# Three conditioned transformer blocks on one core: scores of two heads as row tiles, keys moved by POOL's queue, softmax sums spread inside SBUF

## The chip, the cores and the metric

The kernel runs on one core of a Trainium2 chip. A core has TensorE (PE: matmuls, with a separate load of the stationary operand), VectorE (DVE), ScalarE (ACT), GpSimd (POOL) and SyncE (SP, used here only to start transfers); each follows its own instruction stream, and they meet at semaphores. SBUF holds the working data in 128 partitions, PSUM the matmul results in banks of 2 KB per partition. The metric is the device time of one execution in microseconds.

## The reference

A batch of 16 sequences of 256 tokens with 288 channels, and a condition vector for each. First a rotation of the tokens in a 64-dimensional subspace (the exponential of a skew matrix made from the condition). Then three blocks of one form, with their own weights, all in float32:

```python
ada = silu(c) @ W_ada + b_ada
shift_a, scale_a, gate_a, shift_f, scale_f, gate_f = split(ada, 6)
h = layernorm(x) * (1 + scale_a) + shift_a
q, k, v = split_heads(h @ W_qkv + b_qkv)            # 16 heads of 18 channels
p = softmax(q @ k.T * 18 ** -0.5)                   # 256 x 256 for each head
x = x + gate_a * (merge(p @ v) @ W_proj + b_proj)
h = layernorm(x) * (1 + scale_f) + shift_f
x = x + gate_f * (gelu(h @ W_fc1 + b_fc1) @ W_fc2 + b_fc2)   # hidden width 1152
```

## The kernel before, in words

`prepare` (lines 56 to 1007) computes rotations and modulations, until about 168 us. `layers` then runs 48 half-steps, one for each batch element `b` and layer `l`, with `it = 16 l + b`. Each engine has its own `half_step`, a fixed order written out by hand, and the same four kinds of work lie side by side in it: softmax and weighted values of `it`, QKV and scores of `it + 1`, the norm of `it + 2`, and projection and MLP of `it - 1`.

Products that need float32 accuracy are made of three float32r products of high and low parts (`split`, `channel_steps`): ScalarE or VectorE writes the rounded high part, POOL or VectorE the low part (`low`, L1411). So `qk[0]` and `qk[1]` hold queries and keys of all heads as high and low parts, five tiles of 7 x 18 rows.

Scores need both parts in one contraction. Transfers therefore copy pieces into stacks: `q_stack` holds for a pair of heads (a unit, eight of them) three 36-row pieces (high, low, high), 108 rows; `k_stack` holds the pieces high, high, low for each of the two heads with zeros where the other head's rows are, so it is twice as wide. SP issues all 24 transfers of a half-step (`stacks`): three for queries and six for keys of units 0 to 4 (semaphore `s_stack_a`, after shifted unit 4 of the half-step has been computed), nine and six for units 5 to 7 (`s_stack_b`, after shifted unit 7).

- `score_unit` (L1819): for 128 queries at a time one matmul over 108 rows and 512 columns, both heads at once. VectorE reduces each unit to row maxima (`unit_max`, L2070), which TensorE transposes (L1829); ScalarE negates them, and SP and ScalarE copy them into rows 108 and 109 of `q_stack`, where ones in `k_stack` meet them.
- `shifted_unit` (L1842): keys by queries, four matmuls over 110 rows and 256 columns, the maxima already subtracted. ScalarE takes the exponential of the whole unit (L1604). Two units are in flight, in the two PSUM tiles `scores`.
- `weighted_values` (L1856): four heads as column tiles of 32, with a column of ones that gives the softmax sums in rows 18, 50, 82, 114. ScalarE copies the result to `o_full` (L1611).
- The sums: ScalarE issues a store to DRAM (`gather_sums`, L1618) before GELU 0 and a load into `sums`, 128 partitions of 32 (`load_sums`, L1623), behind it. VectorE takes the reciprocal, ScalarE stores it and issues four broadcasts into `inv_sum`. VectorE writes `o_full * inv_sum` rounded to `o_att[0]` (L2082), POOL computes the same product in full (L1481) and subtracts (L1411) for `o_att[1]`. The projection of the next half-step waits for that.
- The MLP: up-projections 0 to 4 (L1881) alternate between two PSUM banks; GELU `n` makes `g_full` (L1646) and `hidden[0]` (L1647), and up `n + 2` waits for it. `down` (L1736) follows in six parts, with score units between them.

TensorE's order in a half-step: projection of `it - 1` with the maxima's transposes, QK tiles 0 to 2 with shifted units 0 to 2 between, shifted 3, MLP transposes, shifted 4, weighted values 0 and 1, shifted 5 and 6, values 0, shifted 7, up 0, weighted values 2 and 3, up 1, values 1, up 2 and 3, score unit 0, up 4, score unit 1, transposes of `it + 2`, then down parts with score units 2 to 7 between.

Of the kernel before, what the change touches and what calls it, by code (L numbers as in the profile page):

```python
# [12 lines left out]
P = 128  # L13
# [25 lines left out]
PAIR_ROWS, SHIFTED_ROWS = 6 * HD, 6 * HD + 2  # L39
# [20 lines left out]
def prepare(nc, dram, keep, early):  # L60
# [10 lines left out]
    with ExitStack() as ctx:  # L71
# [264 lines left out]
        def _(act):  # L336
# [26 lines left out]
            def constant_stacks():  # L363
# [5 lines left out]
                for u in (0, 4):  # L369
                    A(k_stack[:, u:u + 4, :, :].rearrange("p u n t -> p (u n t)"),  # L370
                      one[:, 0:1].to_broadcast([P, 8 * T]), ACT.Copy, scale=0.0).then_inc(early["s_kinit"], 1)

            def constant_rows():
                act.wait_ge(early["s_kinit"], 2)
                act.wait_ge(s_ident, 16)
                k_stack, rows = early["k_stack"], slice(P - 32, P)
                for par in range(2):
                    for u in (0, 4):
                        A(k_stack[rows, u:u + 4, par, :], one[rows, 0:1].unsqueeze(2).to_broadcast([32, 4, T]), ACT.Copy,
                          scale=ident[rows, PAIR_ROWS + par:PAIR_ROWS + par + 1]).then_inc(early["s_kinit"], 1)  # L380
# [72 lines left out]
            for k in range(PHASES):  # L453
# [3 lines left out]
                if k == 1:  # L457
                    constant_rows()
# [551 lines left out]
def layers(nc, dram, keep):  # L1010
    dram["sum_scratch"] = nc.dram_tensor("sum_scratch", (4, 2 * 512), F32, kind="Internal").ap()

    ident, mods = keep["ident"], keep["mods"]
    with ExitStack() as ctx:  # L1014
# [20 lines left out]
        k_stack = sb("k_stack", [P, H // 2, 2, T], F32R)  # L1035
# [34 lines left out]
        s_stack_b = sem("s_stack_b")  # L1070
        s_v_ps = sem("s_v_ps")
# [10 lines left out]
        s_sum_st = sem("s_sum_st")  # L1082
# [5 lines left out]
        s_o_norm = sem("s_o_norm")  # L1088
# [42 lines left out]
        def qkv_order(tile, rows_as_given):  # L1131
# [3 lines left out]
            if rows_as_given:  # L1135
                pairs = qk_part.rearrange("p (b c) -> p b c", c=PAIR)
                return [pairs[:, 0:5, :], pairs[:, 8:13, :], pairs[:, 5:7, :], pairs[:, 13:16, :],
                        pairs[:, 7, :].rearrange("p (a c) -> p a c", c=HD), tile[:, 2 * C:3 * C]]
            tiles = qk_part.rearrange("p (m c) -> p m c", c=QK_ROWS)
            return [tiles[:, 0:5, 0:PAIR], tiles[:, 0:5, PAIR:2 * PAIR], tiles[:, 0:2, 2 * PAIR:3 * PAIR],  # L1140
                    tiles[:, 2:5, 2 * PAIR:3 * PAIR], tiles[:, 0:2, 3 * PAIR:QK_ROWS], tile[:, V_START:IN_COLS]]

        def conversion(n, rows, part=None):
# [4 lines left out]
            blocks = slice(0, 6) if part is None else slice(0, 5) if part == "qk" else slice(5, 6)  # L1148
# [76 lines left out]
        def qk_rows_of(m):  # L1225
            return QK_ROWS if m < 2 else 3 * PAIR
# [1084 lines left out]
```

## Time and profile before

| | |
|---|---|
| median of 3 runs | 2104.65 us (2098.85 to 2105.66) |
| the profiled execution | 2105.64 us, span 2103.9 us |
| mean granted clock of TensorE | 0.969 |
| busy: PE, PE loads | 1967.8 us (94%), 1754.2 us (83%) |
| busy: DVE, ACT, POOL | 1210.3, 1120.0, 1003.5 us |
| `unit_max` L2070 | 384 of 1222 ns |
| exponentials L1604 | 384 of 1027 ns |
| score matmuls L1819, shifted L1842 | 768 and 1536 |
| POOL's full product L1481 | 96 of 1479 ns |
| transfer packets on POOL's queue | 2256, 7.17 MB |

Busy times are the union of an engine's instructions; issues of transfers are not counted in them. Matmuls are pipelined, so a matmul's duration (0.28 us for one of 256 columns) is longer than the distance between two of them, and the distance between starts, or between ends, is what one costs. "Idle before" says how long an engine stood still and what released it. A granted clock of 1.00 is 2.4 GHz, 0.5 is 1.2 GHz.

### The profile page before, as it was taken

What the parts mean: (1) busy time and instruction counts of PE and PEld (TensorE: products, weight loads), DVE (VectorE), ACT (ScalarE), POOL (GpSimd) and SP (SyncE); (2) the same over time, 40 slices, a digit from 0 to 9 for tenths busy, and PEclk for the clock granted to TensorE, in tenths of its full rate; (3) what the DMA queues carried; (4) which work ended last, traced back from release to release, by engine and by line L of the source; (5) the groups of instructions that cost most, each with busy time, mean ns of one, the idle gap of its engine ahead of it and who ended that gap; (6) DMA issues with size and microseconds to landing.
All of it is one profiled execution on the core that took longest, in us unless ns stands there. A gap on an engine that the chain in (4) does not pass through costs nothing. (4 is left out here: it accounts for less than half of the span.)

```text
span 2103.9 us, 49860 instructions
## 1 busy us (share of the span) xinstructions
PE 1967.8 (94%) x16599; PEld 1754.2 (83%) x16599; DVE 1210.3 (58%) x2720; ACT 1120.0 (53%) x1932; POOL 1003.5 (48%) x1031
## 2 busy tenths in 40 slices
PE   4785799999999999899999999999999999999997
PEld 2553589999899988789899899998789998998986
DVE  6874466546556475556556465575565565564641
ACT  4232455564655645554655656645555656656552
POOL 1002345545455554645455454554655554554534
PEclk9797899999999999999999999999999999999998
DMA  6523443332333323432333323333433323333320
GB/s 171 139 79 118 126 117 87 100 99 80 104 89 94 99 78 105 146 106 78 108 93 90 95 84 105 97 82 101 137 89 90 98 81 106 96 90 93 86 80 26
DMA packets 138971, 207.34 MB, mean 99 GB/s; under 512 B 35700, under 2 KB 96274, under 8 KB 137822
## 3 DMA queue, kind: packets, MB, share of 16 engines
q1 hardware_dynamic: 111582, 169.78, 29.0%
q10 hardware_dynamic: 25040, 29.18, 4.9%
q0 software_dynamic: 2256, 7.17, 1.3%
q8 instruction: 53, 0.87, 0.2%
q14 instruction: 40, 0.33, 0.0%
HBM read 99.51 MB, written 20.82 MB: 57 GB/s over the span
## 5 line engine op out<-in xcount | busy, mean ns | idle before, releaser
L2070 DVE TENSOR_REDUCE maxima<-scores 128x4 f32<-128x1024 f32 x384 | 460.4, 1222 | 186.1 <-PE scores L1819 181.0
L1411 POOL TENSOR_TENSOR hidden<-g_full,hidden 128x512 fp32r<-128x512 f32 (+1 forms) x240 | 280.4, 1177 | 358.4 <-ACT hidden L1647 357.1
L1604 ACT ACTIVATE probs<-scores 128x1024 f32<-128x1024 f32 x384 | 383.1, 1027 | 95.4 <-PE pv_ps L1856 56.8
L1881 PE MATMUL mlp_ps<-h_mlp,w_up 128*128 128x256 f32 (+1 forms) x3024 | 410.0, 288 | 9.5 <-ACT hidden L1647 5.4
L1881 PEld LDWEIGHTS mlp_ps<-h_mlp,w_up 128*128 128x128 f32 (+1 forms) x3024 | 381.0, 190 | 40.4 <-issue 20.1
L1736 PE MATMUL mlp_ps<-w_down,hidden 128*128 128x288 f32 x2592 | 388.8, 295 | 0.0
L1736 PEld LDWEIGHTS mlp_ps<-w_down,hidden 128*128 128x128 f32 x2592 | 369.4, 188 | 18.1
L1819 PE MATMUL scores<-k_stack,q_stack 108*128 108x512 f32 x768 | 241.3, 406 | 20.8 <-DMA k_stack<-qk 18.2
L1842 PE MATMUL scores<-q_stack,k_stack 110*128 110x256 f32 x1536 | 245.7, 292 | 3.6 <-ACT probs L1604 2.4
L1842 PEld LDWEIGHTS scores<-q_stack,k_stack 110*128 110x128 f32 x1536 | 207.8, 191 | 32.5 <-issue 18.9
L1594 ACT ACTIVATE neg_max<-att_ps 16x256 fp32r<-16x256 f32 x48 | 17.9, 373 | 387.3 <-PE att_ps L1829 387.3
L1481 POOL TENSOR_TENSOR o_full<-o_full,inv_sum 128x512 f32<-128x512 f32 x96 | 140.2, 1479 | 156.9 <-DVE o_att L2082 156.9
L1646 ACT ACTIVATE g_full<-mlp_ps 128x512 f32<-128x512 f32 (+1 forms) x240 | 133.7, 557 | 130.1 <-PE mlp_ps L1881 65.1
L2075 DVE RECIPROCAL inv_few<-sums 128x32 f32<-128x32 f32 x48 | 16.9, 353 | 320.8 <-DMA sums<-sum_scratch 320.8
L1411 POOL TENSOR_TENSOR h_mlp<-h_full,h_mlp 128x512 fp32r<-128x512 f32 x48 | 72.3, 1507 | 261.0 <-DVE h_mlp L2036 260.9
L1856 PE MATMUL pv_ps<-probs,v_sb 128*32 128x256 f32 x3072 | 188.9, 387 | 0.5 <-ACT probs L1604 0.5
L1736 PE MATMUL mlp_ps<-w_out,o_att 128*128 128x288 f32 x1152 | 173.2, 301 | 4.8 <-issue 3.7
L1736 PEld LDWEIGHTS mlp_ps<-w_out,o_att 128*128 128x128 f32 x1152 | 159.6, 191 | 6.6 <-issue 4.0
L1819 PEld LDWEIGHTS scores<-k_stack,q_stack 108*128 108x128 f32 x768 | 128.2, 194 | 33.1 <-DMA k_stack<-qk 19.9
L1793 PE MATMUL att_ps<-h_att,w_in 128*126 128x256 f32 (+3 forms) x1008 | 139.1, 286 | 7.0 <-POOL h_att L1411 5.3
L1856 PEld LDWEIGHTS pv_ps<-probs,v_sb 128*32 128x32 f32 x3072 | 90.7, 111 | 65.6 <-issue 3.8
L1793 PEld LDWEIGHTS att_ps<-h_att,w_in 128*126 128x126 f32 (+3 forms) x1008 | 129.0, 186 | 7.8 <-issue 6.7
(230 smaller groups left out, 2849.6 us busy)
## 6 DMA issues: line engine op xcount, KB each, us to landing
q_stack<-qk SPq DMA_DIRECT2D x144, 180.0 KB
k_stack<-qk SPq DMA_DIRECT2D x288, 90.0 KB
inv_sum<-inv_scratch ACTq DMA_DIRECT2D x192, 128.0 KB, 2.6
k_stack<-qk SPq DMA_DIRECT2D x288, 54.0 KB
x_mid<-out_x SPq DMA_DIRECT2D x48, 288.0 KB, 4.2
out_x<-x_out SPq DMA_DIRECT2D x48, 288.0 KB, 3.1
x_in<-out_x SPq DMA_DIRECT2D x47, 288.0 KB, 3.9
q_stack<-qk SPq DMA_DIRECT2D x144, 72.0 KB
```

The lines of the kernel that those rows point to most:

```text
L1411: tt(out, full, high.bitcast(F32), ALU.subtract).then_inc(signal, 1)
L1481: tt(o_full[:, half, :], o_full[:, half, :], inv_sum[:, half, :], ALU.mult).then_inc(s_o_norm, 1)
L1594: evict(neg_max[:, :], att_ps[0:H, 0:T], ACT.Copy, scale=-1.0).then_inc(s_neg, 1)
L1604: evict(probs[:, u % 4, :, :, :], scores[u % 2][:, :, :, :], ACT.Exp, scale=SCALE)\
L1646: evict(g_full[:, n % 2, 0:width], bank[:, 0:width], ACT.Gelu_apprx_tanh).then_inc(s_gelu, 1)
L1736: last = mm(out, a(left), c(weights[w]), start=start and n == 0, stop=stop and n == total - 1)
L1793: last = mm(qk_bank[n][0:cols.stop - cols.start, (m % 2) * T:(m % 2 + 1) * T], w[:, cols], h, start=count == 0, stop=count == 6)
L1819: last = mm(scores[u % 2][:, qt, :, :], q_stack[r, u, qt * P:(qt + 1) * P], k_stack[r, u, :, :], start=True, stop=True)
L1842: last = mm(scores[u % 2][:, par, kt, :], k_stack[r, u, par, kt * P:(kt + 1) * P], q_stack[r, u, :], start=True, stop=True)
L1856: last = mm(pv_ps[32 * i:32 * i + 32, (g % 2) * T:(g % 2 + 1) * T], v_sb[:, kt, 4 * g + i, :], probs[:, u % 4, i % 2, kt, :], start=kt == ...
L1881: last = mm(up_bank[n % 2][:, (m % 2) * T:(m % 2 + 1) * T], w[:, m * P:(m + 1) * P], h, start=count == 0, stop=count == 6)
L2070: nc.vector.tensor_reduce(out=maxima[:, :, :, u], in_=scores[u % 2][:, :, :, :], axis=AX.X, op=ALU.max).then_inc(s_max, 1)
```

## The change

Queries and keys are stacked by head: rows 0 to 53 for the even head of a unit and 64 to 117 for the odd one (`R` is 64), in both stacks, so that `k_stack` needs no zeros and half the width. A score or shifted unit is four matmuls of 256 columns over 54 or 55 rows, alternately at row position 0 and 64, in two PSUM banks. Units come in pairs, and a pair waits for both units of the pair before. The sixth to eighth units' rows lie elsewhere in `qk`, so the weight blocks are cut otherwise. SP issues 15 transfers (all queries), POOL 12 (all keys). The sums go by four transfers from SBUF to SBUF, all before GELU 0. VectorE writes the full product in place, ScalarE rounds it (`high_o`), POOL only subtracts; the product stands behind `unit_max` 3 in place of 2.

```diff
-        k_stack = sb("k_stack", [P, H // 2, 2, T], F32R)
+        k_stack = sb("k_stack", [P, H // 2, T], F32R)
...
-        PIECES_A, PIECES_B = 16 * 9, 16 * 15
+        PIECES_A, PIECES_B, KEYS = 16 * 6, 16 * 9, 16 * 6
...
+        def head_into_stack(engine, stack, j, par, part, src, row, units, signal):
+            first = R * par + HD * j
+            engine.dma_start(stack[first:first + HD, units, :].bitcast(F32),
+                             qk[part][row:row + HD, src, :].bitcast(F32)).then_inc(signal, 16)
...
             def stacks(it, first=False):
                 hold(s_qk_lo, 3 * it + 3)
                 if not first:
                     hold(s_st, 8 * it - 3 + PRE)
                 for j in range(3):
-                    into_stack(j, Q_PARTS[j], slice(0, 5), slice(0, PAIR), slice(0, 5), s_stack_a)
-                for j in range(3):
                     for par in range(2):
-                        head_into_stack(j, par, K_PARTS[j], slice(0, 5), PAIR + HD * par, slice(0, 5), s_stack_a)
+                        head_into_stack(sp, q_stack, j, par, Q_PARTS[j], slice(0, 5), HD * par, slice(0, 5), s_stack_a)
                 hold(s_st, 8 * it + PRE)
                 for j in range(3):
...
+                    head_into_stack(sp, q_stack, j, 0, Q_PARTS[j], slice(2, 5), 3 * PAIR, slice(5, 8), s_stack_b)
+                    head_into_stack(sp, q_stack, j, 1, Q_PARTS[j], slice(0, 2), 2 * PAIR, slice(5, 7), s_stack_b)
+                    head_into_stack(sp, q_stack, j, 1, Q_PARTS[j], slice(0, 1), 2 * PAIR + HD, slice(7, 8), s_stack_b)
...
 # POOL, half_step
                 if after_next:
                     inverse_deviation(0, it + 2)
+                if after:
+                    first_keys(it + 1)
+                    last_keys(it + 1)
...
                 for half in range(2):
-                    pool.wait_ge(s_o, 2 * it + half + 1)
-                    tt(o_full[:, half, :], o_full[:, half, :], inv_sum[:, half, :], ALU.mult).then_inc(s_o_norm, 1)
-                for half in range(2):
-                    pool.wait_ge(s_o_norm, 2 * it + half + 1)
+                    pool.wait_ge(s_o_hi, 2 * it + half + 1)
                     low(o_att[1][:, half, :], o_full[:, half, :], o_att[0][:, half, :], s_o_lo)
...
+            def first_keys(it, first=False):
+                pool.wait_ge(s_qk_lo, QK_USES * it + QK_USES)
+                pool.sem_inc(s_tick[1], 1)
+                if not first:
+                    pool.wait_ge(s_st, 8 * it - 3 + PRE)
+                    pool.sem_inc(s_tick[1], 1)
+                for j in range(3):
+                    for par in range(2):
+                        head_into_stack(pool, k_stack, j, par, K_PARTS[j], slice(0, 5), PAIR + HD * par, slice(0, 5), s_key_a)
+
+            def last_keys(it, first=False):
+                if not first:
+                    pool.wait_ge(s_st, 8 * it + PRE)
+                    pool.sem_inc(s_tick[1], 1)
+                for j in range(3):
+                    for par in range(2):
+                        head_into_stack(pool, k_stack, j, par, K_PARTS[j], slice(2, 5), 2 * PAIR + HD * par, slice(5, 8), s_key_b)
...
 # ScalarE
             def gather_sums(it):
                 act.wait_ge(s_o_full, 2 * it + 2 + PRE)
-                act.dma_start(dram["sum_scratch"], o_full[HD:P:32, :, :].rearrange("i h t -> i (h t)"))\
-                   .then_inc(s_sum_st, 16)
-
-            def load_sums(it):
...
+                for i in range(4):
+                    row = 32 * i + HD
+                    act.dma_start(sums[32 * i:32 * i + 32, :],
+                                  o_full[row:row + 1, :, :].rearrange("i h t -> i (h t)")).then_inc(s_sum, 16)
+
+            def high_o(it):
+                for half in range(2):
+                    act.wait_ge(s_o, 2 * it + half + 1)
+                    evict(o_att[0][:, half, :], o_full[:, half, :], ACT.Copy).then_inc(s_o_hi, 1)
...
-                for n in range(3):
-                    if after:
-                        qk_high(it + 1, n)
-                    if n < 2:
-                        exponentials(it, n)
+                if after:
+                    qk_high(it + 1, 0)
+                exponentials(it, 0)
+                exponentials(it, 1)
+                if after:
+                    qk_high(it + 1, 1)
+                    qk_high(it + 1, 2)
...
                 gather_sums(it)
                 if before:
                     gelu(it - 1, 0)
-                load_sums(it)
...
+                high_o(it)
                 if after_next:
                     attention_modulate(it + 2, (0, 1, 2), None if before else it + 2, it if before else None)
...
 # TensorE
-            def score_unit(it, u):
+            def score_units(it, u):
...
+                for v in (u, u + 1):
+                    for qt in range(2):
+                        for par in range(2):
+                            r = slice(R * par, R * par + HEAD_ROWS)
+                            last = mm(scores[v % 2][:, par, qt, :], q_stack[r, v, qt * P:(qt + 1) * P],
+                                      k_stack[r, v, :], start=True, stop=True, tile_position=(R * par, 0))
+                    last.then_inc(s_score, 1)
...
-            def shifted_unit(it, u):
+            def shifted_units(it, u):
...
+                else:
+                    pe.wait_ge(s_exp, 8 * it + u + PRE_EXP)
+                for v in (u, u + 1):
                     for kt in range(2):
...
+                        for par in range(2):
+                            r = slice(R * par, R * par + HEAD_ROWS + 1)
+                            last = mm(scores[v % 2][:, par, kt, :], k_stack[r, v, kt * P:(kt + 1) * P],
+                                      q_stack[r, v, :], start=True, stop=True, tile_position=(R * par, 0))
+                    last.then_inc(s_st, 1)
...
 # VectorE
-                    tt(o_att[0][:, half, :], o_full[:, half, :], inv_sum[:, half, :], ALU.mult).then_inc(s_o, 1)
+                    tt(o_full[:, half, :], o_full[:, half, :], inv_sum[:, half, :], ALU.mult).then_inc(s_o, 1)
...
                 for u in range(8):
-                    if u == 3:
+                    if u == 4:
                         normalise(it)
-                    if u == 5 and before:
+                    if u == 6 and before:
                         gate_down(it - 1, 0)
```

TensorE's new order: QK 0, shifted 0 and 1, QK 1 and 2, shifted 2 and 3, MLP transposes, weighted values 0, shifted 4 and 5, weighted values 1, values 0, shifted 6 and 7, up 0, weighted values 2 and 3, up 1, values 1, up 2, scores 0 and 1, up 3 and 4, transposes of `it + 2`, and in the down parts scores 2 and 3, 4 and 5, 6 and 7 ahead of parts 0, 2 and 4.

## Rows read from the trace of the kernel before

**Rows 1.** Table of windows: busy us (instructions) by engine, granted clock, DMA share, GB/s

```profile
1031.97:1069.79 37.82, 37.82 (x321) 34.55 (x319) 21.53 (x41) 21.79 (x36) 19.73 (x21) 1.00 0.34 94
```

**Rows 2.** Line L1829: ns min/median/max, first and last start

```profile
L1829 PE MATMUL att_ps<-ident,maxima x96: 270/272/421, 210.4 to 2035.1; 128*16 128x128 f32 x96
```

**Rows 3.** Waits, whole span: waiter, releaser, us in total, times, longest

```profile
PE scores L1819 <- DMA k_stack<-qk: 18.2, 4, 6.0
PE mlp_ps L1881 <- ACT hidden L1647: 5.4, 8, 1.4
```

**Rows 4.** Timeline of PE, one half-step: start, us, line, operation, count

```profile
1037.04 0.65 PE L1842 MATMUL scores<-q_stack,k_stack 110*128 110x256 f32 x4
1037.52 1.84 PE L1793 MATMUL mlp_ps<-h_att,w_in 128*108 128x256 f32 x14
...
1053.59 3.72 PE L1881 MATMUL mlp_ps<-h_mlp,w_up 128*128 128x256 f32 x28
...
1067.65 1.10 PE L1819 MATMUL scores<-k_stack,q_stack 108*128 108x512 f32 x4
1068.59 1.36 PE L1736 MATMUL mlp_ps<-w_down,hidden 128*128 128x288 f32 x9
```

**Rows 5.** Timeline of ACT with its queue's issues (ACTq), same half-step

```profile
1051.00 0.60 ACT L1611 ACTIVATE o_full<-pv_ps 128x512 f32<-128x512 f32 x1 [0.58 <-PE pv_ps L1856]
1051.49 0.41 ACT L1588 ACTIVATE v_sb<-att_ps 128x288 f32<-128x288 f32 x1
1051.63 0.53 ACTq L1618 DMA_DIRECT2D sum_scratch<-o_full  x1
1052.43 0.60 ACT L1646 ACTIVATE g_full<-mlp_ps 128x512 f32<-128x512 f32 x1 [0.52 <-issue]
1052.92 0.59 ACT L1647 ACTIVATE hidden<-mlp_ps 128x512 fp32r<-128x512 f32 x1
1053.61 0.35 ACTq L1623 DMA_DIRECT2D sums<-sum_scratch  x1
```

**Rows 6.** Timeline of PE in the first stage: tiles of 64 rows

```profile
158.59 0.70 PE L508 MATMUL xt_ps<-u_t,w_rot_x 64*64 64x288 f32 x4
159.23 0.51 PE L696 MATMUL chain_a<-rotations,w_rot_x 64*128 64x288 f32 x1
159.24 0.51 PE L696 MATMUL ps_a<-rotations,w_rot_x 64*128 64x288 f32 x1
159.57 0.40 PE L696 MATMUL chain_a<-rotations,w_rot_x 64*128 64x288 f32 x1
...
159.82 0.40 PE L696 MATMUL chain_b<-rotations,w_rot_x 64*128 64x288 f32 x1
```

**Rows 7.** Timeline of PE, 1006.90 to 1006.95: leaving the column tiles

```profile
1006.58 0.40 PE L1856 MATMUL pv_ps<-probs,v_sb 128*32 128x256 f32 x4
1006.90 0.39 PE L1842 MATMUL scores<-q_stack,k_stack 110*128 110x256 f32 x1
```

**Rows 8.** Issues of transfers by line: ns min/median/max, first and last start

```profile
L1596 ACTq DMA_DIRECT2D q_stack<-neg_max x48: 678/691/1589, 211.4 to 2035.8; - x48
...
L1314 SPq DMA_DIRECT2D k_stack<-qk x576: 764/775/1687, 186.2 to 2026.9; - x192
...
L1633 ACTq DMA_DIRECT2D inv_sum<-inv_scratch x192: 308/438/737, 235.5 to 2059.8; - x192
...
L1158 POOL DMA_DIRECT2D staging<-in_w_up x9: 559/579/664, 170.3 to 1477.6; - x9
```

**Rows 9.** Timeline of POOL, same half-step

```profile
1053.59 1.29 POOL L1411 TENSOR_TENSOR hidden<-g_full,hidden 128x512 fp32r<-128x512 f32 x1 [6.11 <-ACT hidden L1647]
...
1066.36 2.53 POOL L1411 TENSOR_TENSOR o_att<-o_full,o_att 128x512 fp32r<-128x512 f32 x2
```

**Rows 10.** The page's costliest groups: busy us, mean ns, idle before

```profile
L2070 DVE TENSOR_REDUCE maxima<-scores 128x4 f32<-128x1024 f32 x384 | 460.4, 1222 | 186.1 <-PE scores L1819 181.0
...
L1604 ACT ACTIVATE probs<-scores 128x1024 f32<-128x1024 f32 x384 | 383.1, 1027 | 95.4 <-PE pv_ps L1856 56.8
```

More of the change, by code:

```diff
@@ L368, in constant_stacks @@
                     .then_inc(early["s_init"], 1)
[L369 to L380, printed above, removed]
+                A(k_stack[:, :, :].rearrange("p u t -> p (u t)"), one[:, 0:1].to_broadcast([P, H // 2 * T]), ACT.Copy)\
+                    .then_inc(early["s_kinit"], 1)
             def high_weights(n):
@@ L1070, in layers @@
         s_stack_b = sem("s_stack_b")
+        s_key_a = sem("s_key_a")
+        s_key_b = sem("s_key_b")
         s_v_ps = sem("s_v_ps")
@@ L1304, in load_x_in @@
                 sp.dma_start(x_in[:, :, :], dram["out"][b]).then_inc(s_xin, 16)
-            def into_stack(j, part, src, rows, units, signal):
-                sp.dma_start(q_stack[PAIR * j:PAIR * j + PAIR, units, :].bitcast(F32),
-                             qk[part][rows, src, :].bitcast(F32)).then_inc(signal, 16)
-            def head_into_stack(j, par, part, src, row, units, signal, key=True):
-                dest = slice(PAIR * j + HD * par, PAIR * j + HD * par + HD)
-                stack = k_stack[dest, units, par, :] if key else q_stack[dest, units, :]
-                sp.dma_start(stack.bitcast(F32), qk[part][row:row + HD, src, :].bitcast(F32)).then_inc(signal, 16)
-            Q_PARTS, K_PARTS = (0, 1, 0), (0, 0, 1)
             def stacks(it, first=False):
@@ L1831, in maxima_transposes @@
                 last.then_inc(s_max_ps, 1)
[L1833 removed]
+            def shifted_units(it, u):
                 if u == 0:
                     pe.wait_ge(s_neg_st, 32 * it + 32 + 16)
[L1837 to L1840 removed]
+                else:
+                    pe.wait_ge(s_exp, 8 * it + u + PRE_EXP)
+                for v in (u, u + 1):
                     for kt in range(2):
[L1842 to L1844 removed]
+                        for par in range(2):
[3 more added lines that the diff above has]
+                    last.then_inc(s_st, 1)
             def weighted_values(it, g):
@@ L1914, in prologue @@
                 attention_transposes(1)
-                for u in range(8):
-                    score_unit(0, u)
+                for u in range(0, 8, 2):
+                    score_units(0, u)
             def half_step(l, b):
```

99 lines of the change are left out of this document (40 added, 59 removed).

## The prediction

> **What bounds the kernel now.** I read one half-step (one batch element in one layer, 1031.97 to 1069.79 us) out of the middle of the run. The table of windows shows TensorE busy for all 37.82 us of it at clock 1.00, and every other engine busy for 20 to 22 us [rows 1]. The two transposes of L1829 open the half-steps: 48 pairs from 210.4 to 2035.1 us, so a half-step is 38.8 us in the mean [rows 2]; 38 of the 47 steps lie between 37.5 and 38.0 us, and nine at the layer borders take 38.5 to 47 us. The waits say what TensorE stands still for: the key transfers at the start (18.2 us in 4 waits) and ScalarE's `hidden` (5.4 us in 8) [rows 3]. That second wait shows no microsecond in the steady state and yet it binds. In the timelines, up-projection 2 starts at 1053.59, and the `hidden` tile that it needs, begun at 1052.92, ends 0.59 us later, at 1053.51 [rows 4, 5]. TensorE and ScalarE arrive there together. Whatever ScalarE loses before that tile, TensorE loses too.
>
> **TensorE's stream.** A shifted unit (four 256-column matmuls) takes 1037.52 − 1037.04 = 0.48 us, so 0.12 each; two score units (four of 512) take 1068.59 − 1067.65 = 0.94 us [rows 4]. Afterwards each unit is four 256-column matmuls in alternating row tiles. That such tiles overlap, the first stage shows: tiles of 64x128 on partitions 0 to 63 and 64 to 127 start at 159.23 and 159.24, and the next pass follows after 0.25 us for both together [rows 6]. I take 0.12 us for a pair: shifted units 8 x 0.24 = 1.92 us for 3.84, scores 1.92 for 3.76. Removed: 1.92 + 1.84 = 3.76 us a half-step. Bounds: without overlap, at 0.12 us each, the shifted units stay at 3.84 and the scores cost 3.84 for 3.76; with pairs at 0.11, 0.16 us more fall away.
>
> **What changing the tile shape costs.** After the last column-tiled product (ends 1006.58 + 0.40 = 1006.98) the first 128-row matmul ends at 1006.90 + 0.39 = 1007.29: 0.31 us later where the pace is 0.12, so 0.19 lost [rows 7]. Into the row tiles: the 64x64 run ends at 159.29, the first 64x128 at 159.74, which is 0.45 for a pace of 0.24, so 0.21 lost [rows 6]. I take 0.2 us a change; no row shows 128 rows to 64x128 itself, so I keep 0 to 0.25 as ends. The order now has 4 changes a half-step (into and out of the two runs of weighted values). Afterwards it has 20: four shifted pairs, of which one stands between two groups of weighted values, and four score pairs in between up, transposes and down. 16 x 0.2 = 3.2 us come back. Of 3.76 us there stay 0.56: about 0.3 before ScalarE's copy of the second `o` half (four shifted pairs, 8 changes), about 0.25 after up 2. The trips also save a small stall or two before that copy; I take 0.4 there.
>
> The Trainium skill's page TensorEngine Tiling (Array Packing) (Overview, Theoretical Speedup) gives up to 2x for a contraction of at most 64; by that alone the 3.76 us would stay. The same page (Key Properties) says that changing the tiling mode drains the engine. The rows above carry both; the first without the second is rival 2.
>
> **ScalarE ahead of up 2.** This is the step that decides. Now: the `o` copy at 1051.00, `v` at 1051.49, one store of the sums issued at 1051.63 for 0.53 us, GELU 0 at 1052.43 [rows 5]: the issue and its gap hold GELU 0 back by 0.56 us (0.53 and about 0.03). The change issues four transfers in that place, from one partition of `o_full` into 32 of `sums`. No row has that form. Nearest is `q_stack<-neg_max`, on the same queue, inside SBUF, one side in one partition: 0.69 us. SP's key pieces, inside SBUF too, take 0.775; the transfers from DRAM to 32 partitions 0.31 to 0.44 [rows 8]. I take 0.69 + 0.03 = 0.72, 2.88 us for four; ends 0.40 (1.6 us) and 0.80 (3.2 us). So GELU 0 starts 2.88 − 0.56 = 2.32 us later, less the 0.4 us by which TensorE delivers the weighted values earlier: 1.9 us. Values 1 ends earlier too, so TensorE waits at up 2 for some 2.3 us. The load of the sums (0.35 us) falls out behind GELU 0 [rows 5], where ScalarE then has room: no gain. From up 2 on TensorE runs its own order, 0.25 us shorter. Sum per steady half-step: 2.88 − 0.56 − 0.4 − 0.24 = **+1.68 us**.
>
> **The rest, priced at nothing in the steady state.**
> - Keys by POOL: 12 issues at 0.56 to 0.66 (median 0.58) [rows 8] = 7 us, queued behind the two deviation instructions and ahead of `hidden` low. POOL now idles 6.11 us before that product at 1053.59 [rows 9]; with up 2 2 us later they fit, and TensorE reads the first of those products only at down 0. Unhidden they would cost 1 us for each 1 us beyond some 10. SP issues 15 pieces for 24, so the scores' stacks are earlier.
> - Normalisation: VectorE's two products move behind one more maximum (1.22 us) [rows 10], POOL's two products (2 x 1.48 us by the table) become two ScalarE copies of 0.6 us each, one overlapping. The low part now ends at 1068.89 for a half-step, and with it a projection, that starts at 1069.79 [rows 1, 9]; it becomes about 1 us earlier relative to that. If this slack of 0.9 us were lost, the excess would go straight onto the step.
> - QK copies 1 and 2 behind exponentials 0 and 1: the MLP transposes wait for the low part of QK 1. Worked through with 1.03 us an exponential [rows 10], the next one starting 0.1 before the end of the last, it is ready within 0.1 us. Score pairs wait for both maxima of the pair before: 2 x 1.22 us against some 2.5 us of down work, also level; the slack of both is nil, and a tenth missing costs a tenth a half-step.
> - Start-up: the 18.2 us of waits on keys lie in the first two sets of scores [rows 3]. 24 issues in a row become 15 on SP beside 12 on POOL; at 0.78 us that is 18.7 us for 11.7. Behind that the maxima bind. I take 8 us gained (bounds 4 and 12).
>
> VectorE works beside POOL's issues, and no row of before shows what that does to one. The Trainium skill's page SBUF — State Buffer (SBUF: two separate sides, the box on DVE and SWDGE) has a rule against the change: a two-port VectorE operation keeps GpSimd from writing descriptors, about 3.1 us for 0.62. It would make rival 4 likelier.
>
> **Sum.** Own time 2105.64 us (span 2103.9). 38 steady half-steps x 1.68 = 63.8; the nine long ones, where weights bind part of the time, at half: 7.6; start −8. 2105.6 + 63.4 = 2169; the profiled run is 1 us above the median 2104.65, so 2168.
>
> **Rivals.**
> 1. *The four transfers issue cheaply*, at 0.40 us as from DRAM. 1.6 − 0.56 − 0.4 − 0.24 = +0.4 us; 42.5 x 0.4 − 8 = +9: 2115. For it: 32 destination partitions share out evenly as those from DRAM do. Against: both SBUF-to-SBUF rows are 0.69 to 0.78.
> 2. *Changing the tile shape is free* between 128 rows and two times 64 (the other side). Then 1.6 us more fall away behind up 2, but only some 0.5 ahead of it, as the exponentials and the table load bind there. 1.68 − 2.1 = −0.42; 42.5 x −0.42 − 8 = −26: 2080, and with rival 1 about 2025. It becomes faster below some 0.08 us a change. For it: no row has this very pair. Against: both neighbouring forms lost 0.19 to 0.21.
> 3. *The row tiles do not overlap* in this number format. Both halves grow by 1.92 us: 2169 + 42.5 x 3.84 = 2330. Against: rows 6.
> 4. *POOL's issues cost over 1 us each.* 12 x 1.2 = 14.4 us, 4 us beyond the slack, of which half reaches down: +2 x 42.5 = 2250.
>
> **How the numbers follow.** My forecast 0.52, rival 1 0.18, rival 2 0.13 (with 1: 0.04 of it), rival 3 0.04, rival 4 0.07, unnamed 0.06. My forecast's own range is 2145 to 2200 (0.66 to 0.80 us an issue, 0.17 to 0.23 a change). The range 2085 to 2210 holds forecast and rival 1 and leaves out most of rivals 2 to 4. 0.3% is 6.3 us, about what a measurement tells from no change. Faster: rival 2 and a few cheap mixtures, 0.17. Same: the lower edge of rival 1, 0.08. Slower 0.75.
>
> **What would show it.** The profile after: issue durations of the new `sums<-o_full` (0.69 or 0.4); a TensorE wait of the up-projection on ScalarE's `hidden` of about 2 us in some 40 half-steps; two row-tile matmuls starting 10 ns apart; 0.3 us between the ends on either side of a change; half-steps of 39.5 us. A half-step under 37.8 us would refute the sum; with the `hidden` wait present the changes of tile shape are mis-sized, without it the issues are.

## The result, and the profile after

The changed kernel takes 2302.01 us (median of 4, 2295.09 to 2311.84) against 2103.4 us for the kernel before: ratio 1.095, 95% interval 1.091 to 1.100. It is slower, as forecast, but by 199 us in place of 63, and outside the range. The profiled execution has a span of 2300.4 us at a mean granted clock of 0.924; before it was 2103.9 at 0.969. One execution of the later kernel after_filler took 7479.13 us at a mean granted clock of 0.258, as no other did; its median below is that of the other three.

Waits of the changed kernel, whole span (waiter, releaser, us in total, times, longest); compare [rows 3], where the up-projection stood 5.4 us for `hidden` and the keys 18.2:

```profile
DVE inv_few L2089 <- DMA sums<-o_full: 448.8, 48, 14.4
ACT g_full L1658 <- issue: 188.9, 50, 5.2
PE mlp_ps L1899 <- ACT hidden L1659: 156.5, 47, 4.5
```

The first row costs nothing here: VectorE's next work, the maxima, has to wait for the scores in any case (214.2 us in all). The third is the stall at up-projection 2: 3.3 us in each of 47 half-steps. The second names its cause: ScalarE stands 3.8 us before GELU 0 for its own issues.

TensorE in one half-step (1118.57 to 1159.42), to be held against [rows 4]:

```profile
1120.38 1.82 PE L1807 MATMUL att_ps<-h_att,w_in 128*108 128x256 f32 x14
1122.13 0.73 PE L1860 MATMUL scores<-q_stack,k_stack 55*128 55x256 f32 x8
...
1135.20 1.93 PE L1899 MATMUL mlp_ps<-h_mlp,w_up 128*128 128x256 f32 x14
1136.97 1.09 PE L1817 MATMUL att_ps<-w_in,h_att 128*128 128x288 f32 x7
1140.54 3.31 PE L1899 MATMUL mlp_ps<-h_mlp,w_up 128*128 128x256 f32 x14 [2.48 <-ACT hidden L1659]
1143.79 0.84 PE L1836 MATMUL scores<-k_stack,q_stack 54*128 54x256 f32 x8
```

Read the durations of the two up-projections: 14 matmuls took 1.93 us at 1135.20 and 3.31 at 1140.54, behind 2.48 us of idleness. ScalarE and its queue there, for [rows 5]:

```profile
1135.34 0.60 ACT L1619 ACTIVATE o_full<-pv_ps 128x512 f32<-128x512 f32 x1 [0.53 <-PE pv_ps L1874]
1135.83 0.41 ACT L1596 ACTIVATE v_sb<-att_ps 128x288 f32<-128x288 f32 x1
1135.96 3.18 ACTq L1629 DMA_DIRECT2D sums<-o_full  x4
1139.40 0.60 ACT L1658 ACTIVATE g_full<-mlp_ps 128x512 f32<-128x512 f32 x1 [3.17 <-issue]
1139.90 0.59 ACT L1659 ACTIVATE hidden<-mlp_ps 128x512 fp32r<-128x512 f32 x1
```

Windows of the stretch before up 2, of the next 3.46 us, and of the 3.4 us after those (columns as in [rows 1]; the granted clock is the third number from the end):

```profile
1136.00:1140.54 4.54, 2.06 (x17) 1.83 (x15) 0.00 (x0) 1.37 (x4) 2.45 (x5) 1.00 0.59 180
1140.54:1144.00 3.46, 3.46 (x16) 3.23 (x18) 0.35 (x1) 1.35 (x4) 2.50 (x2) 0.51 0.21 62
1144.00:1147.40 3.40, 3.40 (x32) 3.27 (x33) 2.36 (x2) 1.85 (x4) 1.30 (x1) 1.00 0.03 5
```

TensorE idles for half of the first window, and in the second it is granted 1.2 GHz: 16 matmuls where the third window has 32. This second cost of the stall was in no term of the prediction.

Issues by line (ns min/median/max), for [rows 8]:

```profile
L1629 ACTq DMA_DIRECT2D sums<-o_full x192: 552/809/2645, 227.9 to 2249.6; - x192
L1281 SPq DMA_DIRECT2D q_stack<-qk x720: 697/699/2807, 184.2 to 2212.4; - x180
L1281 POOL DMA_DIRECT2D k_stack<-qk x576: 498/518/1963, 186.3 to 2204.8; - x192
```

The longest issues are three to four times the median: on ScalarE and SP an issue is not of one length.

**Where the time is.** The trace's 35 steady half-steps (below 38.0 us before; the prediction counted 38) went from 37.80 to 41.94 us in the mean: 35 x 4.14 = 144.9. The twelve others grew by 50.9 together. The first maxima transposes come at 209.71 for 210.4, the tail is 1.3 us longer. Sum 196.4, the difference of the spans. Times in the half-step, in us from the transposes of L1846 (L1829) on, means of 33 steady ones, read from the timelines of each run (over all 35 they differ by at most 0.06):

| run | second `o` copy | GELU 0 | up 2 | up 2 to end | length | at low clock |
|---|---|---|---|---|---|---|
| before | 17.45 | 18.87 | 20.04 | 17.77 | 37.80 | 0 |
| changed | 16.76 | 21.68 | 22.82 | 19.12 | 41.94 | 4.45 |
| after_filler | 16.75 | 21.64 | 22.82 | 17.54 | 40.36 | 0.10 |
| before_spread | 17.44 | 21.08 | 22.22 | 18.69 | 40.91 | 2.07 |
| after_dram | 16.77 | 18.25 | 19.39 | 20.14 | 39.53 | 1.45 |
| after_sp | 16.77 | 17.55 | 19.34 | 19.39 | 38.73 | 0.41 |

### The profile page after: what moved, and what is told of

Same layout as the page of the kernel before. It is cut to its first block and busy times, and to the rows that moved or that the text cites. A ratio compares the mean times of both kernels' runs of the same rounds, so it can differ in the third digit from the quotient of the medians.

```text
span 2300.4 us, 51795 instructions
## 1 busy us (share of the span) xinstructions
PE 2002.0 (87%) x17367; PEld 1708.6 (74%) x17367; DVE 1201.7 (52%) x2735; ACT 1169.0 (51%) x2026; POOL 1161.5 (50%) x1511
## 5 line engine op out<-in xcount | busy, mean ns | idle before, releaser
L1899 PE MATMUL mlp_ps<-h_mlp,w_up 128*128 128x256 f32 (+1 forms) x3024 | 479.4, 319 | 160.1 <-ACT hidden L1659 156.5
L1899 PEld LDWEIGHTS mlp_ps<-h_mlp,w_up 128*128 128x128 f32 (+1 forms) x3024 | 436.2, 220 | 205.9 <-ACT hidden L1659 167.7
L2084 DVE TENSOR_REDUCE maxima<-scores 128x4 f32<-128x1024 f32 x384 | 452.3, 1220 | 214.3 <-PE scores L1836 214.2
L1750 PEld LDWEIGHTS mlp_ps<-w_down,hidden 128*128 128x128 f32 x2592 | 354.6, 190 | 12.3
L1281 POOL DMA_DIRECT2D k_stack<-qk x576 | 295.7, 529 | 30.4 <-issue 19.0
L1393 POOL TENSOR_TENSOR o_att<-o_full,o_att 128x512 fp32r<-128x512 f32 x96 | 121.9, 1291 | 144.2 <-ACT o_att L1635 144.2
L1836 PE MATMUL scores<-k_stack,q_stack 54*128 54x256 f32 x1536 | 159.4, 332 | 35.8 <-DVE maxima L2084 22.9
L1836 PEld LDWEIGHTS scores<-k_stack,q_stack 54*128 54x128 f32 x1536 | 117.3, 210 | 71.5 <-issue 29.3
L1860 PE MATMUL scores<-q_stack,k_stack 55*128 55x256 f32 x1536 | 144.9, 308 | 4.9 <-ACT probs L1612 3.5
L1807 PE MATMUL att_ps<-h_att,w_in 128*108 128x256 f32 (+3 forms) x1008 | 137.5, 284 | 6.2 <-POOL h_att L1393 5.1
L1860 PEld LDWEIGHTS scores<-q_stack,k_stack 55*128 55x128 f32 x1536 | 105.4, 188 | 49.3 <-ACT probs L1612 29.8
```

The lines of the kernel that those rows point to most:

```text
L1281: engine.dma_start(stack[first:first + HD, units, :].bitcast(F32), qk[part][row:row + HD, src, :].bitcast(F32)).then_inc(signal, 16)
L1393: tt(out, full, high.bitcast(F32), ALU.subtract).then_inc(signal, 1)
L1750: last = mm(out, a(left), c(weights[w]), start=start and n == 0, stop=stop and n == total - 1)
L1807: last = mm(qk_bank[n][0:cols.stop - cols.start, (m % 2) * T:(m % 2 + 1) * T], w[:, cols], h, start=count == 0, stop=count == 6)
L1836: last = mm(scores[v % 2][:, par, qt, :], q_stack[r, v, qt * P:(qt + 1) * P], k_stack[r, v, :], start=True, stop=True, tile_position=(R * ...
L1860: last = mm(scores[v % 2][:, par, kt, :], k_stack[r, v, kt * P:(kt + 1) * P], q_stack[r, v, :], start=True, stop=True, tile_position=(R * ...
```

## The experiments: stall, clock and issues

The theory after this result: four long issues make the stall, the stall makes the low clock, the rest of the change gains. Four kernels; every ratio from here on is to the kernel before on the same chip.

**after_filler**: three idle-time copies of a product whose result they do not change, where TensorE stood still.

```diff
+                    for _ in range(3):
+                        values(it + 1, 1, filler=True)
                     values(it + 1, 1)
```

> The changed kernel with three more copies of the product values 1 (7 matmuls of 288 columns each, 0.95 us) on TensorE ahead of the real one, in the place where it stands still; results are the same, ScalarE's issues stay. Theory A: of the 4.2 us that a half-step got longer some 2.0 come from the stretch at granted clock 0.5 behind the idle time; with 2.85 us of the gap filled the clock stays at 1.00 in most half-steps, and the time falls by 43 x 1.9 = 80 us to about 2220, though TensorE does more work. Rival B: the low clock has another cause (work or power elsewhere): it stays, and the time is 2302 to 2330, as the filler overshoots the gap in some half-steps.

Measured: 2228.73 us (2225.40 to 2239.97), ratio 1.063 (1.059 to 1.067), clock 0.964: theory A. That is 73 us less than the changed kernel (ratio 1.095), though TensorE has more to do. Up 2 starts at 22.82 as in the changed kernel, but in the windows the gap is full and the clock stays:

```profile
1142.00:1145.25 3.25, 3.25 (x26) 3.25 (x26) 0.00 (x0) 1.29 (x3) 2.31 (x6) 1.00 0.57 160
1145.25:1148.75 3.50, 3.50 (x32) 3.23 (x32) 0.82 (x2) 2.16 (x5) 2.95 (x3) 1.00 0.22 64
```

So the low clock follows the idleness, and costs 19.12 − 17.54 = 1.58 us a half-step. The Trainium skill's page TensorE: Matmul & The Clock Gate (Part 1: The HAM clock gate) says that idleness gates the clock to 1.2 GHz; the rows agree. What is left behind up 2, 17.54 for 17.77, is 0.23 us shorter than before (forecast: 0.24). Row tiles and order stand together in it; no run separates them.

**before_spread**: the kernel before with nothing but the new gather.

```diff
-                act.dma_start(dram["sum_scratch"], o_full[HD:P:32, :, :].rearrange("i h t -> i (h t)"))\
...
+                for i in range(4):
+                    row = 32 * i + HD
+                    act.dma_start(sums[32 * i:32 * i + 32, :],
+                                  o_full[row:row + 1, :, :].rearrange("i h t -> i (h t)")).then_inc(s_sum, 16)
```

> The kernel before with only the gather changed: four transfers from SBUF to SBUF ahead of GELU 0. Theory A: the issues cost as in the changed kernel, some 4.1 us, so GELU 0 starts 3.5 us later, TensorE waits 3.5 us ahead of up 2, and 3.4 us or more at granted clock 0.5 follow, which cost another 1.7 to 2.2: +5.3 us in the steady half-step, about 2104 + 43 x 5.3 = 2330 us. Rival B: the issues after the first are long only because POOL issues its twelve key transfers in the same microseconds; here they take 0.56 to 0.66 us as in the long half-steps, 2.6 in all: GELU 0 2.0 us later, clock fall included +3.7 us, 2265 us. Rival C: an idle time of 2 us does not bring the clock down by itself: +2 us a half-step, 2190.

Measured: 2241.02 us, ratio 1.067 (1.065 to 1.069). Rival B, with 24 us less than its number. Its issues, and TensorE and the windows at up 2:

```profile
L1620 ACTq DMA_DIRECT2D sums<-o_full x192: 563/639/942, 229.2 to 2188.1; - x192
```

```profile
1071.38 5.11 PE L1878 MATMUL mlp_ps<-h_mlp,w_up 128*128 128x256 f32 x28 [2.10 <-ACT hidden L1645]
```

```profile
1068.10:1071.35 3.25, 1.19 (x10) 0.95 (x8) 0.20 (x1) 1.10 (x3) 0.00 (x0) 1.00 0.28 72
1071.35:1074.85 3.50, 3.47 (x16) 3.47 (x17) 0.15 (x1) 1.44 (x4) 2.52 (x2) 0.52 0.15 41
```

Without POOL's key transfers an issue takes 0.64 us, not 0.81, and never 2.6. From `o` copy to GELU 0 it is 3.64 us for 1.42: +2.22, where the prediction had +2.32. In the changed kernel it is 4.92, which is 1.28 us more. That these belong to POOL's transfers is only argued here; spread_keys_sp, below, tests it. This one part, with the low clock behind it, makes seven tenths of the loss: 141 us over its own runs of before (2099.79), of 199.

**after_dram** and **after_sp**: the changed kernel without issues ahead of GELU 0; the first with the old store and load, the second with the four transfers on SP.

```diff
 # after_dram: gather_sums
-                for i in range(4):
...
+                act.dma_start(dram["sum_scratch"], o_full[HD:P:32, :, :].rearrange("i h t -> i (h t)"))\
 # after_sp: between the two groups of query transfers
+                if not first:
+                    gather(it - 1)
                 hold(s_st, 8 * it + PRE)
```

> The changed kernel with one part undone: the sums go to DRAM by one store ahead of GELU 0 and come back by one load behind it, as before. Theory A: the four issues between the second o copy and GELU 0 (mean some 4.1 us in all, for 0.53 before) make TensorE stand still ahead of up-projection 2, and the idle time is followed by a stretch at granted clock 0.5; the other parts of the change gain. In the trace of the changed kernel up 1 ends 0.7 us earlier in the half-step than before, and what follows up 2 would be 0.7 us shorter without the stretch at half clock. So 37.8 - 1.4 = 36.4 us a half-step and 2104 - 60 = 2045 us (2030 to 2060), with no stall at up 2 and clock 1.00 in the steady state. Rival B (the terms of the prediction): row tiles, keys and normalisation together gain only 0.4 + 0.24 us a half-step, start-up 1 us: 2075 us. Rival C: the keys on POOL or the pair waits cost what is not seen beside the stall: 2100 or above.

> The changed kernel with the four transfers of the sums issued by SP, between its query transfers for units 0 to 4 and those for units 5 to 7. Theory A: nothing stands between o copy, v copy and GELU 0 on ScalarE, so the stall and the low clock go, and GELU 0 comes 0.56 us earlier than with one store: 0 to 0.5 us a half-step better than the run with the DRAM store, 2025 to 2045 us. The sums arrive some 4 us behind the o copy; if they come later than ScalarE reaches the store of the inverses, the stall moves there. Rival B: the last query transfers, now behind the sums, are late for scores 4 and the time is 2060 or above.

Measured: 2191.91 us, 1.043 (1.041 to 1.046), and 2141.82 us, 1.019 (1.018 to 1.021). Up 2 comes at 19.4 in both, as expected. What follows is no gain, against my theory: other waits appear (rival C of the first, rival B of the second). The wait for the store of the sums, before and in after_dram:

```profile
ACT g_full L1646 <- DMA sum_scratch<-o_full: 31.7, 43, 1.2
ACT g_full L1662 <- DMA sum_scratch<-o_full: 135.9, 43, 4.8
```

It has become (135.9 − 31.7) / 43 = 2.4 us longer, for the same store. In after_sp it is the query transfers behind the sums, and GELU 2, which needs POOL's first low part, queued behind twelve issues:

```profile
ACT g_full L1665 <- POOL hidden L1404: 96.4, 52, 6.4
PE scores L1843 <- DMA q_stack<-qk: 29.5, 35, 7.5
```

## The experiments: the key transfers

New theory: POOL's key transfers, priced at nothing, delay every other transfer in flight and ScalarE's and SP's issues.

**before_keys_pool**, **spread_keys_sp**, **dram_keys_sp** and **dram_keys_split** vary who issues the keys:

```diff
 # before_keys_pool: on the kernel before;  the opposite in spread_keys_sp and dram_keys_sp, on the changed one
-                        head_into_stack(j, par, K_PARTS[j], slice(0, 5), PAIR + HD * par, slice(0, 5), s_stack_a)
...
+                    first_keys(it + 1)
+                    last_keys(it + 1)
 # dram_keys_split: first keys by SP, last keys by POOL
                         hidden_low(it - 1, n)
+                        if n == 0 and after:
+                            last_keys(it + 1)
```

> The kernel before with one part of the change: POOL issues the twelve key transfers (twice as many destination rows' width as in the change, zeros stay), at the place that the change gives them. Theory A: the store of the sums to DRAM lands 2 to 3 us later, as it shares the DMA engines with the keys, ScalarE waits for it ahead of GELU 1, TensorE at up 3; the low parts of hidden come later. +1.5 to +2.5 us a half-step, 2165 to 2210 us. Rival B (as predicted): POOL has the room, nothing waits for it, SP's own queue is shorter: 2095 to 2105.

Measured: 2186.51 us, 1.040 (1.037 to 1.042). Theory A, with a smaller delay than it had: from the issue of the store to that of the load it is 3.4 us for 2.0 before (means of the 35 steady half-steps), and up 3 starts 22.9 to 23.4 us into the half-step for 21.8. POOL's issues are short, yet the kernel before loses 85 us by them alone. What got longer here is the landing: the store's own issue took 0.53 us as before, and SP's twelve query issues beside POOL's took 9.0 us in sum, also as before. So POOL's transfers do not lengthen every issue. The two parts tried alone cost 141 and 85 us, together more than the 199 of the whole change.

> The changed kernel with SP issuing all keys; ScalarE issues the four transfers of the sums as in the change. Theory A: without POOL's transfers under way the issues take 0.56 to 0.66 us, 2.5 in all (4.1 in the changed kernel), as in the run before_spread; GELU 0 is 1.5 us earlier than in the changed kernel, the clock falls in fewer half-steps, the last keys are late by about 1 us: 40 us a half-step, 2190 to 2230 us. Rival B: it is the engine's place in the queues, not POOL's transfers, that makes them long: unchanged 4.1 us, 2300.

Measured: 2281.87 us, 1.085 (1.079 to 1.090), between the two numbers. The issues shortened as theory A has it:

```profile
L1629 ACTq DMA_DIRECT2D sums<-o_full x192: 554/629/897, 230.8 to 2232.3; - x192
```

From `o` copy to GELU 0 it is 3.50 us for 4.92 (means of the 35): without POOL's transfers 1.42 us of the changed kernel's time there are gone, much like the 1.28 above. It is not the mere number of transfers, either: SP issues all 27 of the stacks between 10.0 and 30.3 us, and ScalarE's four, from 17.4 to 20.0, lie in the middle of them and stay short. But the gain went to the scores, which now wait for keys (79.7 us in 45 times).

> The run with the sums through DRAM, with a second part undone: SP issues all 27 transfers of the stacks and POOL none. The run after_dram stood at 39.5 us a half-step: up-projection 2 came 0.65 us early as it should, but ScalarE then stood 3 us ahead of GELU 1 for the store of the sums to land, and TensorE at up 3. Theory A: it is POOL's key transfers, under way at the same time, that slow that landing (and made the issues of the four transfers long); with them on SP the store lands as in the kernel before, and what comes behind up 2 shortens by some 2.5 us. But SP now needs 27 x 0.70 = 18.9 us from 10.0 us into the half-step on, until 29, and scores 4, wanted at 28, wait for the last keys some 3 us: 38.5 to 39 us a half-step, 2125 to 2150 us, with the wait now at scores 4 on a DMA. Rival B: the landing is slow whoever issues; the wait ahead of GELU 1 stays and the scores' is added: 2200 or above. Rival C: neither binds: 36.4 us, 2045.

Measured: 2269.15 us, 1.081 (1.078 to 1.083). The first half of theory A holds: the wait for the store of the sums fell from 135.9 to 37.0 us. The second was far too small: SP issues until 30.3 us, and scores 4 start at 31.95 where 28 was wanted; the low clock follows here too (clock 0.925).

```profile
PE scores L1841 <- DMA k_stack<-qk: 149.6, 50, 6.6
```

In the kernel before, SP's last issue ends hardly earlier, at 30.0 us, and no steady half-step waits for it: there the last keys are needed for scores 5, which start at 32.4. In pairs, scores 4 and 5 need them together, at 28. This earlier demand, by 4 us, is in no term of the prediction.

> The sums through DRAM; SP issues all queries and the keys of units 0 to 4, POOL the six transfers of the last keys, behind its first low part of hidden. Theory A: when the store of the sums is under way (17.4 to 19 us into the half-step) POOL has no transfer in flight, so the store lands as before; SP is done at 10 + 21 x 0.7 = 24.7 and POOL at about 23.5, before scores 4 wants them at 28. So the whole gain of row tiles and order shows: 36.4 to 36.8 us a half-step, 2045 to 2065 us. Rival B: three transfers of hidden low come late behind POOL's 3.1 us of issues and TensorE waits in down: 2080 to 2110. Rival C: late stores again: 2150 or above.

Measured: 2129.99 us, 1.014 (1.012 to 1.016), 38.0 us a half-step without low clock: the best version with row tiles, and nearest to rival B, whose mechanism it has (20 us above its range; the steady half-step lost only 0.2 us, the twelve others together 15.6). The store lands in time (35.6 us in all), but GELU 3 needs a buffer that POOL's second low part frees, and that part stands behind six issues:

```profile
ACT g_full L1668 <- POOL hidden L1398: 123.1, 48, 4.2
```

**Repairs**: after_behind and behind_split move ScalarE's four issues behind GELU 1; dram_keys_early and behind_split let POOL issue only the last keys, 13.8 us into the half-step; serial_tiles is behind_split with both matmuls of one head first (`for par` outside `for qt`).

```diff
 # after_behind, behind_split: ScalarE
-                gather_sums(it)
...
                     gelu(it - 1, 1)
                 if after:
                     v_evict(it + 1, 1)
+                gather_sums(it)
 # dram_keys_early, behind_split: POOL; SP issues the first keys
-                    first_keys(it + 1)
                     last_keys(it + 1)
 # serial_tiles: both kinds of unit
-                    for qt in range(2):
-                        for par in range(2):
+                    for par in range(2):
+                        for qt in range(2):
```

> The changed kernel with ScalarE's four issues moved behind GELU 1 and the second v copy (the store of the inverses then stands behind GELU 3, their spreading behind GELU 4); all twelve key transfers stay on POOL. Theory A: the stall ahead of up-projection 2 and the half clock behind it were 2.8 + 1.6 us of the half-step and go, so up 2 starts at 19.3; the issues now stand in ScalarE's pause before GELU 2, which they overrun by 1 to 2 us, and POOL's first low part of hidden, behind the twelve issues, ends 21.2 us into the half-step and holds GELU 2 as well: 37.5 to 38.5 us a half-step, 2095 to 2150 us. Rival B: the issues cost TensorE the same wherever they stand before up 4: 39 us or more, 2170 or above. Rival C: the sums come 3 us later and the projection waits for the normalised values: 2150 or above, with that wait in the table.

> Sums through DRAM, keys of units 0 to 4 by SP, the six transfers of the last keys by POOL at the place of the change, 13.8 us into the half-step, ahead of the low parts of hidden. Theory A: six issues end at 16.9, before the store of the sums at 17.4, so the store lands nearly as before, and POOL is free for the first low part at 19.4, which removes the wait of GELU 3 for POOL that cost 2 us when they stood behind that part: 36.2 to 36.8 us a half-step, 2040 to 2065 us. Rival B: the six transfers still delay the store's landing by 1 us or more: 37.2 us and above, 2085 or more.

> Both repairs at once: the four SBUF-to-SBUF transfers of the sums behind GELU 1, keys of units 0 to 4 by SP and the last six by POOL at 13.8 us. Theory A: ScalarE reaches GELU 0 and 1 without any issue or wait for a store; the four issues, 0.6 us each without POOL's transfers under way, take 20.1 to 22.6 us and hold GELU 2 some 1.3 us, up 4 some 0.5: 36.5 to 37.2 us a half-step, 2050 to 2080 us. Rival B: the later inverses hold the projection: 2100 or above.

Measured: 2217.57 us (1.056, 1.054 to 1.058), 2165.15 (1.030, 1.028 to 1.032), 2212.97 (1.053, 1.051 to 1.056). All three missed theory A. In all up 2 starts at 19.3 to 19.4, and all lose it behind: in after_behind and behind_split the inverses come later, VectorE blocks on them ahead of the maxima, and scores wait (87.8 and 70.7 us). With the early keys, in dram_keys_early and behind_split, SP's six key issues beside POOL's take 5.1 and 4.9 us in sum instead of 4.2 (means of the 35), and scores 0 wait for keys (69.0 and 75.5 us). In dram_keys_early the load of the sums also comes at 21.35 for 19.59 in dram_keys_split, so its rival B was right: six early transfers still delay the store. The row of dram_keys_early:

```profile
PE scores L1845 <- DMA k_stack<-qk: 69.0, 42, 3.1
```

> As behind_split, but within a unit both matmuls of the even head come first and then both of the odd head, so that neighbours mostly use the same rows of the array. It prices the overlap of row tiles. Theory A: only the middle two of four matmuls can overlap, 3 paces of 0.12 us for a unit where alternation takes 2, in each of 16 units: +1.9 us a half-step at most, of which that behind up 2 counts in full: 2110 to 2160 us. Rival B: the tiles do not overlap at all in either order, or the chip overlaps across more than one: no difference to behind_split within 10 us.

Measured: 2219.67 us, 1.058 (1.055 to 1.060), within 7 us of behind_split. In both traces all matmuls of the shifted units start in twos, at most 12 ns (behind_split) and 19 ns (serial_tiles) apart, and the shifted units end alike (up 0 at 12.90 and 12.95). So rival B, in its second form: the overlap doesn't depend on alternation within four matmuls.

**keys_behind_low2** and **keys_half**: POOL's last keys behind the third low part; all six, or three with the others on SP.

```diff
-                        if n == 0 and after:
+                        if n == 2 and after:
                             last_keys(it + 1)
 # keys_half only
-                    for par in range(2):
+                    for par in (1,):
```

> As dram_keys_split (sums through DRAM, SP issues queries and the keys of units 0 to 4, 38.0 us a half-step), but POOL issues its six last key transfers behind the third low part of hidden, not behind the first. In that run GELU 3 waited until 25.2 us for the second low part, 1.5 us longer than for up 3. Theory A: that wait goes, GELU 3 starts at 23.7, the first down part at 25.9 instead of 27.4; POOL issues from 23.9 to 27.0, the last keys land at 29 and scores 4, wanted at 28.4, wait about 0.6 us; no transfer of POOL's is in flight beside the store of the sums. 37.0 to 37.6 us a half-step, 2065 to 2095 us, the first version with the row tiles that is not slower than the kernel before. Rival B: the wait at scores 4 is 2 us and more, with the low clock behind it as in dram_keys_sp: 2130 or above.

> As keys_behind_low2, but POOL issues only three of the six last key transfers and SP the other three behind its queries. Theory A: POOL is done at 25.4 us, its last low parts come 1.5 us earlier, SP is done at 27.4 and its pieces land at 28.5 to 29: 36.9 to 37.4 us a half-step, 2060 to 2085 us. Rival B: POOL's three transfers in flight stretch SP's issues (as with the early ones, 4.2 us for six became 4.8) and scores 4 wait 1.5 us or more: 2100 or above.

Measured: 2224.16 us (1.058, 1.056 to 1.060) and 2246.52 (1.069, 1.066 to 1.072). The first is its rival B, with 2.8 us of every steady half-step at low clock. In it the last issue ends at 26.9 us, and scores 4 start at 31.0:

```profile
1074.56 0.74 PE L1847 MATMUL scores<-k_stack,q_stack 54*128 54x256 f32 x8 [2.66 <-DMA k_stack<-qk]
```

I had allowed 2 us for landing; it took 4. keys_half has the time of its rival B and not the mechanism: SP's 15 query issues took 10.6 us in sum, as in dram_keys_sp without POOL's; SP ends at 28.2, and scores 4 start at 31.6. None of the places tried for the keys is free: early they delay the sums and the first keys, in the middle POOL's low parts, late the scores. No version with row tiles beat the kernel before.

## Why the prediction was wrong, point by point

The mean half-step was to grow by 1.68 us and grew by 4.14. Two steps failed. The clock behind the stall was no term (1.58 us). The key transfers on POOL were "priced at nothing", and beside them ScalarE's four issues cost 1.28 us more. Against these 2.86 us stand 0.39 on the other side: the `o` copy came 0.29 us earlier than forecast, and the issues alone were 0.10 cheaper. The direction was right, and for the reason given.

- **What binds** (ScalarE ahead of up 2): right. The wait predicted at some 2 us is there, at 3.3.
- **TensorE's stream**: right in its sum, but the 0.12 us for a pair was not read from [rows 6]: at granted clock 1.00 the pairs there follow each other after 0.25 us, twice that. The price proved right here, for the other form; that was luck. (Its bound for pairs at 0.11 counts 16 pairs; there are 32.) The eight matmuls of a shifted pair end 0.66 us after the last 128-row one (1120.38 + 1.82 = 1122.20, 1122.13 + 0.73 = 1122.86); four pairs at 0.115 are 0.46, so 0.20 went into the change of shape. Predicted 0.12 and 0.2. Rivals 2 and 3 are refuted. The rule that changing the tiling mode drains the engine (the Trainium skill, TensorEngine Tiling (Array Packing), Key Properties) agrees with these 0.20 us.
- **Ahead of the `o` copy** −0.4: it was −0.69. **Behind up 2** −0.24: it was −0.23 where the clock stays.
- **Four issues** +2.32: right for the issues alone (+2.22), wrong in the changed kernel (+3.50), because the step "keys by POOL: 7 us hidden" looked for their price on POOL. There it holds: 12 issues in 6.06 us, medians of 0.518. The price stands on the other queues. Rival 4 (POOL's issues over 1 us) is refuted as a price of every issue: the mean of the 576 is 0.529. The rule that stood beside it (the Trainium skill, SBUF — State Buffer, SBUF: two separate sides) is not refuted by that, since 387 of them ran while VectorE did nothing. The five longest, 0.89, 0.89, 1.69, 1.69 and 1.96 us, all ran beside copies of new weights on VectorE and ended 0.10 us after the last copy; sixteen others beside such copies took 0.50 to 0.58. In these five the trace agrees with the rule; they make some 4.5 us of the whole run.
- **The clock**: no term, and this is the step that cost most. "TensorE waits at up 2 for some 2.3 us" was priced as 2.3 us; the idleness brings 1.58 us more.
- Sum per steady half-step: −0.69 + 3.50 + 1.35 (−0.23 and 1.58) = +4.16, measured 4.14, predicted 1.68. The prediction took 38 half-steps for steady; the trace has 35, and twelve others.
- **Long half-steps** at half the price: they lost 4.2 us each, the full price. **Start-up** −8: it was −0.7. In before_keys_pool, with the keys alone moved, it was −7.8; in the changed kernel SP's issues stretch to over 2 us beside POOL's, the first scores come at 196.70 for 193.73, and from there each pair takes 3.26 us because it waits for both maxima:

```profile
196.70 1.22 PE L1836 MATMUL scores<-k_stack,q_stack 54*128 54x256 f32 x8 [8.06 <-DMA q_stack<-qk]
199.95 1.22 PE L1836 MATMUL scores<-k_stack,q_stack 54*128 54x256 f32 x8 [2.02 <-DVE maxima L2084]
```

- **Normalisation** at nothing: right. The low part ends at 1154.70, the projection starts at 1157.83.

What stays open: by which mechanism POOL's transfers lengthen the issues of another queue, and why they do so in the changed kernel and not in before_keys_pool.

## What to carry to other kernels

A stall of TensorE can cost more than itself (here 1.58 us more, behind stalls of 3.3): look at the granted clock behind it, and add a term. A transfer moved to an idle engine is not hidden because its issues are; price what else is in flight at that moment, issue by issue and landing by landing. Working in pairs brings forward the moment at which the second unit's data are needed. Where a kernel is level in several places, an edit that gains 0.9 us in one and moves transfers is paid back at the next.

## What the hardware showed that was not expected

- Each of the four issues on ScalarE's queue took 0.63 to 0.64 us in the median without POOL's transfers in flight and 0.81, up to 2.65, with them. SP's 15 query issues took 12.8 us in sum in the changed kernel and 10.6 in dram_keys_sp. SP's twelve in before_keys_pool were not lengthened (9.0 us). The Trainium skill's page DMA: Bandwidth & Descriptors (Rules for kernel authors) says that spreading transfers over the issuing engines gives no bandwidth and only saves issue time; here even the issue time was not all saved.
- In before_spread stalls of 1.9 to 2.1 us were followed by half clock in some half-steps and not in others (2.07 us at low clock in the mean). In after_dram a stall of 1.55 us, until 560.47, was followed by it too: the clock was 1.00 from 558.0 to 561.5 us and 0.50 from 561.6 to 565.0.
- Row tiles of the two heads overlap in either order of issue (2212.97 and 2219.67 us), and a pair of them takes 0.115 us.
- Five of POOL's 576 issues took 0.89 to 1.96 us beside copies on VectorE, and ended 0.10 us after them; the median is 0.518.
